# Turning the gathered slot rows by permuting loads and 32-by-32 block transposes in a fused attention and mixture-of-experts layer

## The chip, the core and the metric

The kernel runs on one core of a Trainium2 chip. Its metric is device time in microseconds, the median of several executions: 1471.43 us before the change, from three runs (1471.36 to 1472.84).

The core has five engines with queues of their own: TensorE (matrix products, from SBUF into PSUM), VectorE, ScalarE, GpSimd and SyncE, which here only issues transfers. They wait for each other through semaphores alone, and all of these waits are written out by hand.

## The reference

```python
x = layernorm(x + attention(x))          # 4 sequences x 512 tokens x 512 channels, 16 heads of 128
x_flat = x.reshape(2048, 512)
router_logits = x_flat @ w_router        # 8 experts
top_vals, top_idx = top_k(router_logits, 2)
probs = softmax(top_vals)
w_tok = zeros(2048, 8).at[rows, top_idx].add(probs)
h = square(relu(einsum("nc,ecd->ned", x_flat, w_fc)))     # every expert 512 x 512
y = einsum("ned,edc->nec", h, w_proj)
x = layernorm(x + einsum("nec,ne->nc", y, w_tok))
```

Attention has RMS norms on queries and keys, an ALiBi bias and a causal mask, a softmax, an RMS norm of the result and an output projection. The change touches only the experts' part. The inputs are fp32.

## The kernel before

**Attention** takes the first 965 us or so. After it comes **routing** in steps of 128 tokens (`token_steps`, 16 of them): project, add the residual, normalize, turn the tokens, route, rank within the expert. Each token's row is sent by GpSimd's indirect transfers (`dispatch`, line 952) to two slots of `slots_x` in HBM, and its two gate weights to `slots_g`.

**Slots.** A slot tile is 128 rows of 512 channels, all of one expert. Each expert has a region of tiles. 39 slot tiles are worked through (`SLOT_TILES`), expert by expert in "turns". The first turn belongs to the head expert, which is chosen after eight token tiles; its first two tiles (`HEAD`) are worked through while the last tokens are still being routed.

Precision: products are fp32r, with every fp32 operand split into a high part (ScalarE rounds it) and a low part (VectorE or GpSimd subtracts), and three products for each pair of blocks. So the product of a slot tile with a 512x512 matrix is 12 products of 128x128 by 128x512 (`times`, line 1641).

One slot step `k` has this order on the engines (`slot_step` in each of the functions `slots_*`):

- TensorE: turn the hidden rows of `k` (four identity products), the up product of tile `k+1`, turn the slot rows of tile `k+2` (`turn_x`, line 1635: four identity products into `turn_ps`), the down product of `k`.
- ScalarE: round the turned hidden rows of `k` (L1463), rectify the up product of `k+1` into `relu` (L1459), round the turned slot rows of `k+2` (`round_x`, L1454), scale the down product of `k` by the gates (L1469).
- VectorE: low part of the hidden rows of `k` (L1525), square of `k+1` (L1521, from `relu` and `relu` in SBUF), low part of the slot rows of `k+2` (`split_x`, L1516, from PSUM and `xt_hi`).
- SyncE: when the rows of `k+2` are turned, load the slot rows of `k+4` (`load_rows`, L1322, one transfer of 256 KB); then, when the output of `k` is ready, store it to `slots_y` (L1360) and load gates (L1325). The slot rows `xs` have two buffers.
- GpSimd: for each expert from the second on, load the raw weights (L1377) and the weights again as the later high part (L1383), 2 MB each, wait for both, and compute the low part in eight operations (L1392). A raw buffer holds one expert. After the last expert it gathers from `slots_y` into `x1` with indirect, adding transfers (L1422): 16 token tiles for the slot that comes first, then 16 for the second, each second pair of gathers after the output rows that it needs are stored (`rows_stored`, line 1414).

**The seam** between head and loop: VectorE computes tables of where each tile lies and which expert owns it (`slot_tables`), then `gates`, `row_shifts` (12 chained small operations, lines 1532 to 1548), `split_x(0, 3)`, `row_places` (lines 1554 to 1570), `square(0, 3)` and `split_x(1, 4)`. GpSimd begins to split the second expert's weights when `row_places` has ended (`slots_known`). SyncE loads tiles 2 and 3 when the tables are known and all dispatches have landed.

In the profile a tile's name is that of the first tensor at its place: `y_raw` holds `xs`, the hidden rows and the outputs; `turn_ps` holds the turned slot rows and the up products; `yt_hi` and `yt_lo` hold the high and low parts of slot and hidden rows; `x_nat` is `relu`.

## Time and profile before

| | |
|---|---|
| median of three runs | 1471.43 us (1471.36 to 1472.84) |
| span of the profiled execution | 1469.0 us (no time of its own is given beside it) |
| TensorE busy | 1428.9 us (97%), 7998 products |
| VectorE busy | 771.4 us (53%) |
| ScalarE busy | 727.3 us (50%) |
| GpSimd busy | 415.4 us (28%) |
| mean granted TensorE clock | 0.995 of full speed |
| slot row loads | 39 of 256 KB |
| transfers, share of 16 DMA engines | 31.2% hardware queue (SyncE), 12.0% software queue (GpSimd) |

The span runs from the first to the last instruction. The shares are means over stages with quite different limits: the DMA engines, for example, are 96% busy from 1386 to 1452 us and at 0.34 in the first 1030 us.

### The profile page before, as it was taken

What the parts mean: (1) busy time and instruction counts of PE and PEld (TensorE: products, weight loads), DVE (VectorE), ACT (ScalarE), POOL (GpSimd) and SP (SyncE); (2) the same over time, 40 slices, a digit from 0 to 9 for tenths busy, and PEclk for the clock granted to TensorE, in tenths of its full rate; (3) what the DMA queues carried; (4) which work ended last, traced back from release to release, by engine and by line L of the source; (5) the groups of instructions that cost most, each with busy time, mean ns of one, the idle gap of its engine ahead of it and who ended that gap; (6) DMA issues with size and microseconds to landing.
All of it is one profiled execution on the core that took longest, in us unless ns stands there. A gap on an engine that the chain in (4) does not pass through costs nothing. (4 is left out here: it accounts for less than half of the span.)

```text
span 1469.0 us, 26596 instructions
## 1 busy us (share of the span) xinstructions
PE 1428.9 (97%) x7998; PEld 1209.6 (82%) x7999; DVE 771.4 (53%) x1813; ACT 727.3 (50%) x1633; POOL 415.4 (28%) x410
## 2 busy tenths in 40 slices
PE   8999999999999999999999999989999989999994
PEld 6888888888888888888888888878888867888883
DVE  6555655655555655555555565545555563333334
ACT  5665655655656565556565565622222223333334
POOL 1212121212112212122121121103333445345575
PEclk9999999999999999999999999999999999999997
DMA  5243323232323333233323235433348446665699
GB/s 176 77 129 93 107 93 127 86 114 85 115 93 107 111 111 100 100 98 102 108 93 128 93 107 179 144 123 125 136 121 224 123 172 215 253 247 200 211 199 235
DMA packets 86547, 200.45 MB, mean 136 GB/s; under 512 B 15856, under 2 KB 16496, under 8 KB 83184
## 3 DMA queue, kind: packets, MB, share of 16 engines
q1 hardware_dynamic: 75728, 149.66, 31.2%
q0 software_dynamic: 10784, 50.36, 12.0%
q8 instruction: 18, 0.29, 0.1%
q14 instruction: 17, 0.14, 0.0%
HBM read 160.05 MB, written 92.62 MB: 172 GB/s over the span
## 5 line engine op out<-in xcount | busy, mean ns | idle before, releaser
L378 POOL TENSOR_TENSOR small<-small,half 128x4 f32<-128x4 f32 x193 | 194.9, 1010 | 768.8 <-DVE small L408 768.8
L511 DVE CUSTOM_DVE_ANT_0 logit<-score_ps,bias 128x128 f32<-128x128 f32 (+3 forms) x256 | 124.8, 487 | 157.0 <-PE score_ps L650 117.6
L312 ACT ACTIVATE prob<-logit,small 128x128 f32<-128x128 f32 (+3 forms) x256 | 144.2, 563 | 120.5 <-DVE small L511 116.8
L663 PEld LDWEIGHTS y_ps<-vs,prob_t 128*128 128x128 f32 x1280 | 175.0, 191 | 20.4 <-issue 3.7
L663 PE MATMUL y_ps<-vs,prob_t 128*128 (+1 forms) x1280 | 184.7, 275 | 0.3 <-DVE x_now L412 0.3
L319 ACT ACTIVATE prob_t<-prob_ps 128x128 f32<-128x128 f32 (+3 forms) x256 | 111.6, 436 | 54.4 <-PE prob_ps L656 53.4
L894 ACT ACTIVATE yt_hi<-turn_ps,subln 128x512 fp32r<-128x512 f32 x60 | 41.0, 688 | 154.1 <-PE turn_ps L1188 150.2
L656 PE MATMUL prob_ps<-ident,prob 128*128 128x128 f32 x640 | 112.7, 274 | 3.2 <-ACT prob L312 3.0
L576 PE MATMUL v_ps<-w_hi,x_hi 128*128 (+1 forms) x256 | 106.8, 417 | 1.3 <-DVE w_lo L447 1.3
L576 PE MATMUL v_ps<-w_hi,x_lo 128*128 (+1 forms) x256 | 106.3, 415 | 0.0
L576 PE MATMUL k_ps<-w_hi,x_hi 128*128 (+1 forms) x256 | 103.2, 403 | 0.6 <-DVE w_lo L447 0.6
L576 PE MATMUL q_ps<-w_hi,x_hi 128*128 (+1 forms) x256 | 102.4, 400 | 0.7 <-DVE w_lo L447 0.7
L576 PE MATMUL v_ps<-w_lo,x_hi 128*128 (+1 forms) x256 | 102.6, 401 | 0.0
L576 PE MATMUL k_ps<-w_lo,x_hi 128*128 (+1 forms) x256 | 101.7, 397 | 0.0
L576 PE MATMUL k_ps<-w_hi,x_lo 128*128 (+1 forms) x256 | 101.5, 397 | 0.0
L576 PE MATMUL q_ps<-w_hi,x_lo 128*128 (+1 forms) x256 | 101.3, 396 | 0.0
L576 PE MATMUL q_ps<-w_lo,x_hi 128*128 (+1 forms) x256 | 101.1, 395 | 0.0
L1392 POOL TENSOR_TENSOR w_lo<-w_raw,w_hi 128x512 f32 (+1 forms) x56 | 75.1, 1377 | 82.9 <-DMA w_hi<-in_w_experts 79.2
L656 PEld LDWEIGHTS prob_ps<-ident,prob 128*128 128x128 f32 x640 | 79.7, 141 | 14.3 <-ACT prob L312 7.1
L989 DVE SCALAR_TENSOR_TENSOR yt_lo<-turn_ps,subln,yt_hi 128x512 fp32r<-128x512 f32 x60 | 44.7, 749 | 85.3 <-ACT yt_hi L894 83.7
L240 ACT ACTIVATE ksq<-k_ps 128x512 f32<-128x512 f32 x64 | 38.4, 599 | 97.2 <-PE k_ps L576 97.2
L412 DVE TENSOR_TENSOR x_now<-y_ps,small 128x512 f32<-128x512 f32 x65 | 45.0, 692 | 77.4 <-POOL small L378 77.4
(250 smaller groups left out, 3421.5 us busy)
## 6 DMA issues: line engine op xcount, KB each, us to landing
slots_x<-in_zeros SPq DMA_DIRECT2D x64, 512.0 KB, 5.2
y_scratch<-x_now SPq DMA_DIRECT2D x65, 256.0 KB, 2.9
x_raw<-in_x_t SPq DMA_DIRECT2D x64, 256.0 KB, 2.8
slots_y<-in_zeros SPq DMA_DIRECT2D x64, 256.0 KB, 5.1
y_raw<-y_scratch SPq DMA_DIRECT2D x14, 1024.0 KB
w_raw<-in_w_experts POOLq DMA_DIRECT2D x7, 2048.0 KB
w_hi<-in_w_experts POOLq DMA_DIRECT2D x7, 2048.0 KB
w_raw<-in_w_all SPq DMA_DIRECT2D x16, 768.0 KB, 6.5
```

The costliest lines, as they stand in the source:

```text
L240: nc.scalar.activation(out[:, :, 0:D], src[:, :].rearrange("p (h d) -> p h d", h=HG), ACT.Square, scale=float(D) ** -0.5).then_inc(done, 1)
L312: nc.scalar.activation(prob[:, 0:width], logit[:, 0:width], ACT.Exp, scale=-1.0, bias=least[:, h:h + 1], accum_out=row_sum[:, (i % 2) * HG ...
L319: nc.scalar.activation(prob_t[:, 0:width], prob_ps[:, 0:width], ACT.Copy)\
L378: nc.gpsimd.tensor_tensor(r, ms, half[:, :], ALU.pow).then_inc(ready, 1)
L412: nc.vector.tensor_tensor(heads(out), heads(src[:, :]), r.unsqueeze(2).to_broadcast([P, HG, D]), ALU.mult).then_inc(done, 1)
L511: nc.vector.tensor_tensor_reduce(out=logit[:, 0:width], in0=score_ps[:, 0:width], in1=bias[:, h, T - width:T], scale=1.0, scalar=3e38, op0 ...
L576: mm = nc.tensor.matmul(out[:, :], xs, ws, start=(s == 0), stop=(s == 3 * CT - 1))
L656: mm = nc.tensor.transpose(prob_ps[:, j * P:(j + 1) * P], prob[:, j * P:(j + 1) * P], ident[:, :])
L663: mm = nc.tensor.matmul(y_ps[:, h * D:(h + 1) * D], prob_t[:, j * P:(j + 1) * P], one(vs[:, bass.ds(now, 1), j, h * D:(h + 1) * D]), start ...
L894: nc.scalar.activation(yt_hi[:, g, :], turn_ps[g][:, :], ACT.Copy, scale=subln[:, 0:1])\
L989: nc.vector.scalar_tensor_tensor(yt_lo[:, g, :], turn_ps[g][:, :], subln[:, 0:1], yt_hi[:, g, :], ALU.mult, ALU.subtract).then_inc(yt_read ...
L1392: nc.gpsimd.tensor_tensor(lo, w_raw[:, s, :], hi, ALU.subtract).then_inc(we_split, 1)
```

## The change

The slot rows no longer go through TensorE. A tile's load becomes four transfers, one for each quarter `u` of the channels. The transfer `u` puts into partition `32u + j` the 128 channels of quarter `u` of the rows `j`, `32 + j`, `64 + j` and `96 + j`. VectorE then transposes 32-by-32 blocks within each group of 32 partitions (`nc.vector.transpose`), and writes the blocks in the order that makes columns of 128 consecutive tokens (`turned_columns`). Partition `32u + j'` of column block `h` now holds channel `128u + 32h + j'`, so the up weights are laid out in that order on the host. The turned rows lie in a new SBUF tile `xt` in place of two PSUM banks; `round_x` and `split_x` read it there.

The order changes at these places. TensorE's `turn_x` is dropped in the head (twice), at the seam (twice) and in each slot step. VectorE gets it in the head ahead of each `split_x`, at the seam ahead of `row_shifts` and of `row_places`, and in the slot step between `split_hid` and `square`. In the head ScalarE waits for `last_projected` before it rounds the slot rows, since their high part lies where the last projection still reads. SyncE's wait on `xs_turned` is now on VectorE's operation.

```diff
--- before.py
+++ after.py
@@ -18,6 +18,8 @@
 AX = mybir.AxisListType
 
 P = 128
+QB = 4
+QP = P // QB
 B, T, C = 4, 512, 512
 H, D = 16, 128
 EPS = 1e-5
@@ -62,6 +64,11 @@
 def expert_block(e):
 
     return (CT + FT) * ((e + 2) % 3)
+
+
+def turned_columns(ap):
+
+    return ap.rearrange("p (h a j) -> p a h j", h=HG, a=QB)
 
 
 def one(ap):
@@ -849,7 +856,7 @@
 
         y_tiles = y_scratch[1:1 + NHG * NT, :, :].rearrange("(g t) p c -> t p g c", g=NHG)
         x_tiles = x_d.rearrange("(t p) c -> t p c", p=P)
-        x_slots = slots_x.rearrange("(k p) c -> k p c", p=P)
+        x_slots = slots_x.rearrange("(k a j) (u c) -> k u j a c", a=QB, j=QP, u=QB)
         LAST = NHG - 1
 
         def tile_of(tiles, t):
@@ -1272,13 +1279,15 @@
         end_rstd = sb("rstd3", [P, NT])
         minus_mean = sb("minus_mean", [P, NT])
 
-        xt_ps, h_ps = turn_ps[0:2], turn_ps[2:4]
+        h_ps = turn_ps[2:4]
+        xt = sb("xt", [P, 2, C])
         ht_ps, ye_ps = [out_ps[0], x1_ps], [out_ps[1], router_ps]
 
         end_set_up = sem("e_set_up")
         table_done = sem("slot_step")
         slots_known = sem("slots_known")
         g_loaded = [sem(f"g_loaded{y}") for y in range(YB)]
+        last_projected = sem("last_projected")
         we_cast = sem("we_loaded")
         xs_loaded = [sem("xs_loaded0"), sem("xs_loaded1")]
         xs_turned, xt_rounded, xt_ready = sem("xs_turned"), sem("xt_rounded"), sem("xt_ready")
@@ -1319,7 +1328,10 @@
                                      min_val=0, max_val=SPARE_TILE)
 
             def load_rows(at, b):
-                sp.dma_start(xs[:, b, :], rows_of(x_slots[bass.ds(at, 1), :, :])).then_inc(xs_loaded[b], 16)
+                for u in range(QB):
+                    sp.dma_start(xs[u * QP:(u + 1) * QP, b, :].rearrange("p (a c) -> p a c", a=QB),
+                                 x_slots[bass.ds(at, 1), u, :, :, :].rearrange("o j a c -> (o j) a c"))\
+                        .then_inc(xs_loaded[b], 16)
 
             def load_gates(at, y):
                 sp.dma_start(gs[:, y:y + 1], rows_of(g_slots[bass.ds(at, 1), :, :])).then_inc(g_loaded[y], 16)
@@ -1451,7 +1463,7 @@
 
             def round_x(b, count):
                 act.wait_ge(xs_turned, count)
-                nc.scalar.activation(xt_hi[:, b, :], xt_ps[b][:, :], ACT.Copy).then_inc(xt_rounded, 1)
+                nc.scalar.activation(xt_hi[:, b, :], xt[:, b, :], ACT.Copy).then_inc(xt_rounded, 1)
 
             def rectify(b, k):
                 act.wait_ge(up_done, k + 1)
@@ -1469,8 +1481,10 @@
                 nc.scalar.activation(yo[:, y, :], ye_ps[b][:, :], ACT.Copy, scale=gs[:, y:y + 1]).then_inc(yo_ready, 1)
 
             second_weight(NT - 3, 1)
+            act.wait_ge(last_projected, 1)
             round_x(0, 1)
             keep_x1(NT - 2, 0)
+            act.wait_ge(last_projected, 2)
             round_x(1, 2)
             second_weight(NT - 2, 0)
             act.wait_ge(summed, NT - 1)
@@ -1513,8 +1527,14 @@
 
             def split_x(b, count):
                 dve.wait_ge(xt_rounded, count)
-                nc.vector.tensor_tensor(xt_lo[:, b, :], xt_ps[b][:, :], xt_hi[:, b, :], ALU.subtract)\
+                nc.vector.tensor_tensor(xt_lo[:, b, :], xt[:, b, :], xt_hi[:, b, :], ALU.subtract)\
                     .then_inc(xt_ready, 1)
+
+            def turn_x(b, loaded, split=None):
+                dve.wait_ge(xs_loaded[b], loaded)
+                if split is not None:
+                    dve.wait_ge(xt_ready, split)
+                nc.vector.transpose(turned_columns(xt[:, b, :]), xs[:, b, :]).then_inc(xs_turned, 1)
 
             def square(b, count):
                 dve.wait_ge(relu_done, count)
@@ -1573,7 +1593,9 @@
             place(NT - 3, 1, 16 * NT - 64)
             gates(NT - 3, 1)
             layernorm(NT - 2, 0, 16 * NT - 32)
+            turn_x(0, 16 * QB)
             split_x(0, 1)
+            turn_x(1, 16 * QB)
             split_x(1, 2)
             choose(NT - 2)
             add_residual(NT - 1, 1, 8 * NT)
@@ -1586,14 +1608,18 @@
             place(NT - 1, 1, 16 * NT - 32)
             slot_tables(lambda: square(1, 2), lambda: split_hid(1, 1))
             gates(NT - 1, 1)
+            turn_x(0, 32 * QB, 1)
             row_shifts()
             split_x(0, 3)
+            turn_x(1, 32 * QB, 2)
             row_places()
             square(0, 3)
             split_x(1, 4)
 
             def slot_step(k, b, h, y, q):
                 split_hid(b, k)
+                if more(k, 2):
+                    turn_x(b, h * (16 * QB) + 32 * QB, k + 1)
                 if more(k, 1):
                     square(1 - b, k + 2)
                 if more(k, 2):
@@ -1632,12 +1658,6 @@
             scale_mean(NT - 2, NT)
 
         def slots_tensor(pe, project, turn_x1, route, rank, keep_busy):
-            def turn_x(b, loaded):
-                pe.wait_ge(xs_loaded[b], loaded)
-                for c in range(CT):
-                    mm = nc.tensor.transpose(xt_ps[b][:, c * P:(c + 1) * P], xs[:, b, c * P:(c + 1) * P], ident[:, :])
-                mm.then_inc(xs_turned, 1)
-
             def times(out, b, hi, lo, first_block, first=0, last=3 * CT):
 
                 for s in range(first, last):
@@ -1668,12 +1688,10 @@
 
             last = (NT - 1) * NHG
             pe.wait_ge(yt_ready, last + 1)
-            project(1, 0)
-            turn_x(0, 16)
+            project(1, 0).then_inc(last_projected, 1)
             pe.wait_ge(yt_ready, last + 2)
-            project(1, 1)
+            project(1, 1).then_inc(last_projected, 1)
             turn_x1(NT - 2, 0)
-            turn_x(1, 16)
             pe.wait_ge(yt_ready, last + 3)
             project(1, 2)
             route(NT - 2)
@@ -1698,19 +1716,15 @@
             times(ye_ps[0], 0, ht_hi, ht_lo, expert_block(0) + CT, 9, 12).then_inc(down_done, 1)
             pe.wait_ge(run_ready, NT + 1)
             down(1, 0, 1)
-            turn_x(0, 32)
             pe.wait_ge(tables_known, 2)
             second = load_owner(HEAD)
             keep_busy(h_ps[1], 10)
             up(0, second, 3)
-            turn_x(1, 32)
 
             def slot_step(k, b, h, y, q):
                 turn_hid(b, k)
                 if more(k, 1):
                     up(1 - b, load_owner(k + 1), k + 2)
-                if more(k, 2):
-                    turn_x(b, h * 16 + 32)
                 down(b, load_owner(k), k)
 
             slot_steps(pe, slot_step, HEAD)
@@ -1803,7 +1817,8 @@
     w_all = np.concatenate([qkv.transpose(3, 1, 2, 0, 4).reshape(W_ROUNDS, P, 3 * GW),
                             proj[:3 * CT].reshape(CT, 3, P, C).transpose(0, 2, 1, 3).reshape(CT, P, 3 * C)])
 
-    experts = np.concatenate([np.asarray(inputs["L0_ffn_w_fc"]).reshape(E, CT, P, F),
+    up = np.asarray(inputs["L0_ffn_w_fc"]).reshape(E, QB, CT, QP, F).transpose(0, 2, 1, 3, 4).reshape(E, CT, P, F)
+    experts = np.concatenate([up,
                               np.asarray(inputs["L0_ffn_w_proj"]).reshape(E, FT, P, C)], axis=1)
     bases = np.arange(E) * REGION_TILES * P
     floors = bases[:, None] + np.concatenate([[-1], P * np.arange(1, NT)])[None, :]
```

## Rows read from the trace of the kernel before

**Rows 1.** Chain that ended last, 1180 to 1469: start us, us, what

```profile
1317.58 2.79 PE turn_ps L1647 x12
1320.81 2.79 PE out_ps L1647 x12
...
1427.76 2.97 DMA slots_y<-y_raw
```

**Rows 2.** Time line of GpSimd: start us, us, engine, line, operation

```profile
1209.84 10.88 POOL L1392 TENSOR_TENSOR w_lo<-w_raw,w_hi 128x512 fp32r<-128x512 f32 x8 [3.66 <-DVEq L1570]
...
1373.94 10.51 POOL L1392 TENSOR_TENSOR w_lo<-w_raw,w_hi 128x512 f32 x8 [13.51 <-DMA w_hi<-in_w_experts]
1386.64 1.68 POOL L1422 DMA_INDIRECT x<-slots_y,slot_y  x1 [2.19 <-issue]
...
1420.97 1.56 POOL L1422 DMA_INDIRECT x<-slots_y,slot_y  x1 [1.67 <-issue]
...
1427.07 1.54 POOL L1422 DMA_INDIRECT x<-slots_y,slot_y  x1 [2.68 <-issue]
...
1451.06 1.54 POOL L1422 DMA_INDIRECT x<-slots_y,slot_y  x1 [0.30 <-issue]
```

**Rows 3.** Time line of VectorE near the end

```profile
1453.79 0.16 DVE L1615 SCALAR_TENSOR_TENSOR minus_mean<-mean_var,rstd 128x4 f32<-128x4 f32 x1 [1.07 <-POOL rstd L1428]
```

**Rows 4.** Time line of VectorE at 1179

```profile
1178.86 0.55 DVE L1009 TENSOR_SCALAR x_now<-res,mean_var,rstd 128x512 f32<-128x512 f32 x1
```

**Rows 5.** Three lines of code: count, ns min/median/max, first and last start

```profile
L1521 DVE TENSOR_TENSOR y_raw<-x_nat x39: 691/693/1684, 1191.9 to 1443.8; 128x512 f32<-128x512 f32 x39
L1516 DVE TENSOR_TENSOR yt_lo<-turn_ps,yt_hi x39: 676/682/692, 1179.3 to 1437.9; 128x512 fp32r<-128x512 f32 x39
L1392 POOL TENSOR_TENSOR w_lo<-w_raw,w_hi x56: 1259/1292/1753, 1209.8 to 1383.2; 128x512 f32 x40, 128x512 fp32r<-128x512 f32 x16
```

**Rows 6.** Time line of SyncE's queue, loads of slot rows

```profile
1163.96 0.91 SPq L1322 DMA_DIRECT2D y_raw<-slots_x  x2
...
1202.90 1.44 SPq L1322 DMA_DIRECT2D y_raw<-slots_x  x2
```

**Rows 7.** Time lines of TensorE, then VectorE, at the seam

```profile
1205.58 0.66 PE L1638 MATMUL turn_ps<-ident,y_raw 128*128 128x128 f32 x4 [0.68 <-DMA y_raw<-slots_x]
...
1207.97 0.49 PE L1647 MATMUL turn_ps<-w_hi,yt_hi 128*128 x1 [0.23 <-issue]
...
1202.95 0.39 DVE L1532 TENSOR_TENSOR beyond<-slot,bases 128x224 f32<-128x224 f32 x1
...
1205.81 0.25 DVE L1548 SCALAR_TENSOR_TENSOR place_y<-slot,first_ahead,shift 128x32 f32<-128x32 f32 x1
...
1207.58 0.17 DVE L1554 TENSOR_TENSOR slot_y<-place_y 128x16 uint32<-128x16 f32 x1
...
1209.19 0.51 DVE L1568 TENSOR_SCALAR due<-due_f,end_tile 128x16 int32<-128x16 f32 x2
```

**Rows 8.** Time line of one slot step, 1245 to 1250

```profile
1245.86 0.60 PE L1662 MATMUL x_ps<-ident,y_raw 128*128 128x128 f32 x4
...
1246.64 0.59 ACT L1463 ACTIVATE yt_hi<-x_ps 128x512 fp32r<-128x512 f32 x1
...
1247.27 0.69 DVE L1525 TENSOR_TENSOR yt_lo<-x_ps,yt_hi 128x512 fp32r<-128x512 f32 x1 [1.95 <-ACT yt_hi L1463]
...
1249.92 0.69 DVE L1521 TENSOR_TENSOR y_raw<-x_nat 128x512 f32<-128x512 f32 x1 [1.96 <-ACT x_nat L1459]
```

**Rows 9.** DMA queues, 1252:1262 then 1397:1425: packets, MB, share of 16 engines

```profile
q0 software_dynamic: 246, 3.77, 89.6%
q1 hardware_dynamic: 217, 0.41, 11.6%
...
q0 software_dynamic: 1856, 3.38, 74.2%
q1 hardware_dynamic: 1998, 2.35, 26.6%
```

## The prediction

> **What bounds the kernel now.** I read the busy table first: TensorE works 97% of the span at full clock, so the first question is what sets its order. The chain of waits shows it in the slot loop: blocks of 12 products of 2.79 us that start 3.23 us apart [rows 1]. The 0.44 us between them are the four identity products of a turn, one for the hidden rows and one for the slot rows, in alternation. A slot step is therefore 2 x 3.23 = 6.46 us. But the chain leaves TensorE at the end: it goes over a store of slot rows (2.97 us) into GpSimd's gathers. So TensorE's order decides up to about 1427 us and GpSimd's after it, and I read GpSimd's time line next [rows 2]. It begins its first weight split at 1209.84, its seventh at 1373.94 (27.35 us per expert), and its first gather at 1386.64. Those starts follow loads and splits, never TensorE. GpSimd then has some slack: 18 gathers at 1.845 us each take 33.2 us, and the 19th starts at 1427.07, 40.4 us after the first. GpSimd can thus come 7.2 us later before the end moves. Past 1427 it issues without a gap to 1451.06, and VectorE's last statistics had to wait 1.07 us for GpSimd's power behind those gathers [rows 2, 3].
>
> **Filled tiles.** The reference's routing of these inputs gives the experts 5, 4, 5, 4, 4, 5, 5 and 4 tiles, 36 of 39. The head is the third expert, so turns begin at tiles 0, 5, 9, 14, 18, 22, 27 and 32. Tile 33 releases the gather at 1427.07; the last three tiles hold nothing.
>
> **What is removed.** 39 turns of four identity products leave TensorE. Two of them lie before the seam, 2 x 0.44 = 0.9 us, and all that follows the last projection comes 0.9 us earlier. 35 lie in the loop: if TensorE stayed the bound, 35 x 0.44 = 15.4 us.
>
> **What a turn costs on VectorE.** No transpose of VectorE is in the trace. The nearest operations on 128x512 fp32 are 0.55 us (a scale from SBUF to SBUF) and, as the long end, 1.68 us (the slowest squaring) [rows 4, 5]. I take 0.69, an unhindered pass, and keep both ends.
>
> ScalarE's two new waits, on the last projection of the first two head groups, cost nothing: TensorE was past both when it turned these rows, and the rounding came after.
>
> **The seam.** The load of tile 2 is issued at 1202.90, held by the last dispatch, and lands at 1205.58, 2.68 us later [rows 6, 7]. It will be issued at 1202.0. Now it is four transfers, and issues stand about 0.57 us apart (two in 0.91 us, the second lasting 0.34): the fourth leaves at 1203.7 and lands at 1206.4. VectorE has the new turn ahead of row_shifts, and there it waits for the load. The 12 chained small operations of row_shifts (1202.95 to 1206.06), which lay beside the load, come behind it: turn to 1207.1, row_shifts 3.1 us to 1210.2, split to 1210.9, first product at 1211.1. Before, that product stood at 1207.97, so TensorE is 3.1 us late. The second turn is put ahead of row_places (1207.58 to 1209.70, 2.1 us): 1210.9 + 0.7 + 2.1 = 1213.7, and GpSimd, which waits for slots_known, starts splitting at 1213.85 in place of 1209.84. That is 4.0 us on GpSimd's whole chain [rows 2, 7]. TensorE has part of its delay back since the third tile's turn is gone too: I put up(5) at 1229.3 (before 1226.8).
>
> **The loop.** The new step is 0.44 + 2.79 + 2.79 = 6.02 us. On the path from one hidden turn to the up products two halves on, the times behind the end of the hidden turn (1246.46) are: its rounding and split done at +1.5, the new turn at +2.2, the rectified rows at +3.4 (+3.6 with waits), square, split_x [rows 8]. Alone these end at +5.0 of 6.02: hidden. Beside GpSimd's splits they don't. The squaring reads two SBUF tiles and took up to 1.68 us; the splits that read PSUM never exceeded 0.69 [rows 5]. split_x now reads xt and xt_hi, both in SBUF, so it joins the squaring. The squaring starts within a GpSimd operation of 1.29 us and waits half of one; split_x right behind it meets the next one: 3.6 + 1.3 + 1.9 = +6.8 to +7.0. That is 0.9 us late per step, in the 1.8 steps of each split, 7 x 1.8 x 0.9 = 11 us. Of 28 x 0.44 = 12.3 us almost nothing is left, and up(32) is at 1229.3 + 27 x 6.02 + 11 = 1402.8, before 1401.6.
>
> GpSimd pays too. Eight operations at the least 1.259 are 10.07 us; the first split took 10.88 with two squarings within it, so 0.4 us for each [rows 2, 5]. 12.6 more such meetings add 5.4 us. A lower bound is nothing, the upper 0.69 for each.
> By the Trainium skill ("SBUF — State Buffer", section "SBUF: two separate sides") the pair of ports is held for a whole instruction and the loser fully blocks; by that each meeting would cost GpSimd 0.69 us and the sum 8.7 instead of 5.4. The squaring's stretched times agree with a lock, the 0.4 us does not bear out the full length.
>
> **The transfers.** A slot tile was 128 packets of 2 KB; now it is 512 of 512 B. While weights load, both queues are served by packet, not by byte: in 10 us 246 packets of 16 KB on GpSimd's queue and 217 of SyncE's [rows 9]. In the gather stretch too: 1856 beside 1998 in 28 us with the engines full. SyncE's queue has 1998/28 x 6.46 = 461 packets per step; the change adds 384 and 48 completions: 893, at 71 per us 12.5 us, twice a step. In the loop the 16 us between two weight loads clear the backlog, and a load made during one lands when the weights do, within the two steps that it has. For the weights themselves: SyncE's 217 packets took 11.6% of the engines in those 10 us, 0.085 us each; a quarter of the bytes each would free up to 0.9 us per load, twice as many packets' time would add 1.2. I take 0.15 less, 1 us in six loads. SyncE's three more issues per step (3 x 0.57 us) fall where it waits for the output rows, over 3 us a step, and hold nothing.
> The Trainium skill ("DMA: Bandwidth & Descriptors", section "Specifications") gives 512 B as the least transfer at line rate. By it the smaller pieces cost nothing in the stretches where engines are free, and it says nothing of two queues that take turns; by it alone the sum would be that of the first rival below.
>
> **The end, summed.** GpSimd's first gather comes 4.0 + 5.4 - 1.0 = 8.4 us later, at 1395.0. Up(32) at 1402.8 puts the turns of tiles 32, 33, 34 and 35 at 1398.2, 1404.2, 1410.2 and 1416.2, and each releases the load of the tile two on. Tile 34's (issued 1398.2) takes 576/71 = 8.1 us and the landing's 2, so 1408.5: in time. Tile 35's queues behind 288 packets of stores and gates (4.1 us) and takes 8.1 more, so 1421 where 1417.6 would still be hidden (the turn may come 1.4 us late before the squaring wants VectorE). Tile 36's ends with the first list's traffic, at 1432.5. The store of tile 33 (issued 1424.7) stands behind tiles 36 and 37 in the same queue and lands at 1434.5. Gather 19 therefore starts at 1435.5 against 1427.07: +8.4, and the 13 behind it, the statistics and the normalization follow as before. Slots end on VectorE at 1454 (before 1447.8), +6, covered. The profiled span goes from 1469.0 to 1477.4. The profiled execution has no time of its own beside its span; the median run is 2.4 above that span, and the same 2.4 gives 1479.8. I say 1479.
>
> **Rivals.**
> 1. The queue does not starve (four pieces of one row count as one packet, or gathers leave room). Then 8.4 - 7.2 = 1.2 us later: 1472.6. For it: TensorE never waited in that stretch so far. Against: the packet counts are equal in two stretches of very different sizes.
> 2. Faster: split_x does not meet GpSimd (it falls between its operations), or weights come sooner since small packets take less of each turn. GpSimd is then 4.0 late or less, below the 7.2 of slack, and TensorE leads: 2.5 late at up(5), less 12.3, so tile 33 comes 9.8 earlier and the gathers 7.2 - 4.0 = 3.2 earlier: 1468.2. It decides wherever GpSimd's delay stays under 7.2 us.
> 3. All 37 x 0.44 = 16.3 us: 1455. Only if the seam hides too and GpSimd's chain shortens by 9 us or more, for which no row speaks.
> 4. Late loads in the weight stretches as well: a load that is issued as the weights start has 576 packets at 22 per us and comes with the end of the weights, 2 us late, six times: 12 us on top, 1491.
>
> **How the numbers follow.** Forecast 0.45 (its own range 1475 to 1487), rival 1 0.22, rival 2 0.15, rival 3 0.05, rival 4 0.13. What this kernel's measurement can tell from no change is about 0.2%, 2.9 us. Faster by more: rival 3, most of rival 2 and an edge of rival 1, 0.19. Within: most of rival 1, 0.20. Slower: 0.61. The range leaves out rival 3, the far end of rival 2 and the far end of rival 4: 1466 to 1492.
>
> **What would show it.** Right: the first product of tile 2 near 1211, GpSimd's first split near 1213.9; that split at 11.3 us or more; split_x with a maximum near 1.9 us; the turn at 0.7; first gather near 1395; in the gathers GpSimd waiting on a store of slot rows, and VectorE's turn waiting on loads. Wrong: a first gather before 1391, loop blocks at 3.0 us apart throughout, or no wait for slot rows after 1400.

## The result and the profile after

The changed kernel takes 1477.78 us (median of 6 runs, 1476.52 to 1484.32); the kernel before took 1471.74 beside it (1468.96 to 1473.17). The ratio is 1.0052 (95% interval 1.0038 to 1.0066): slower by 0.5%, and 1479 was forecast. The profiled execution took 1481.32 us for a span of 1479.7, so it lies 3.5 above its median. That matters below: its routing ran 1.6 to 1.8 us later than in the trace of before, ahead of anything that changed at the seam (the first load of `x_nat` in routing is at 967.95 against 966.35, the last at 1164.09 against 1162.26).

The page of the changed kernel: the span, busy times, the granted clock in 40 slices, and the chain that ended last by engine.

```profile
span 1479.7 us, 26713 instructions
...
PE 1420.5 (96%) x7842; PEld 1198.3 (81%) x7843; DVE 807.5 (55%) x1852; ACT 728.5 (49%) x1633; POOL 419.5 (28%) x410
...
PEclk9999999999999999999999999999999989999997
```

156 identity products are gone, yet TensorE is only 8.4 us less busy. The new `8` in the clock row is the slice of the seam.

The three lines of code beside [rows 5] (count, ns min/median/max), of the changed kernel:

```profile
L1537 DVE STREAM_TRANSPOSE xt<-y_raw x39: 695/702/714, 1181.2 to 1445.7; 128x512 f32<-128x512 f32 x39
L1530 DVE TENSOR_TENSOR yt_lo<-xt,yt_hi x39: 677/684/1777, 1182.6 to 1448.4; 128x512 fp32r<-128x512 f32 x39
L1404 POOL TENSOR_TENSOR w_lo<-w_raw,w_hi x56: 1253/1293/1782, 1218.3 to 1397.7; 128x512 f32 x40, 128x512 fp32r<-128x512 f32 x16
```

The turn costs 0.70 us, and the split of the slot rows, never over 0.69 before, now reaches 1.78.

GpSimd's time line, beside [rows 2]: start, us, then in brackets the idle time before and what ended it.

```profile
1218.33 10.79 POOL L1404 TENSOR_TENSOR w_lo<-w_raw,w_hi 128x512 fp32r<-128x512 f32 x8 [11.27 <-DVEq L1590]
...
1388.05 10.94 POOL L1404 TENSOR_TENSOR w_lo<-w_raw,w_hi 128x512 f32 x8 [13.16 <-DMA w_hi<-in_w_experts]
1401.17 1.68 POOL L1434 DMA_INDIRECT x<-slots_y,slot_y  x1 [2.19 <-issue]
...
1414.09 1.53 POOL L1434 DMA_INDIRECT x<-slots_y,slot_y  x1 [2.03 <-issue]
...
1438.05 1.54 POOL L1434 DMA_INDIRECT x<-slots_y,slot_y  x1 [0.86 <-issue]
...
1462.03 1.54 POOL L1434 DMA_INDIRECT x<-slots_y,slot_y  x1 [0.30 <-issue]
```

The first split is 8.5 us later than before, the first gather 14.5, the nineteenth and the last 11.0. The pause of 2.03 us ahead of the seventh gather fits a wait for TensorE's rows, though the view names no releaser: it starts 5.6 us behind the issue of a store (1408.47), as the nineteenth does (1432.45).

**The seam.** SyncE's issues of tiles 2 and 3, then VectorE's time line beside [rows 7]:

```profile
1204.11 4.90 SPq L1332 DMA_DIRECT2D y_raw<-slots_x  x8
```

```profile
1211.15 0.71 DVE L1537 STREAM_TRANSPOSE xt<-y_raw 128x512 f32<-128x512 f32 x1 [7.07 <-DMA y_raw<-slots_x]
1211.78 0.35 DVE L1552 TENSOR_TENSOR beyond<-slot,bases 128x224 f32<-128x224 f32 x1
...
1214.59 0.25 DVE L1568 SCALAR_TENSOR_TENSOR place_y<-slot,first_ahead,shift 128x32 f32<-128x32 f32 x1
1214.88 0.69 DVE L1530 TENSOR_TENSOR yt_lo<-xt,yt_hi 128x512 fp32r<-128x512 f32 x1
1215.48 0.70 DVE L1537 STREAM_TRANSPOSE xt<-y_raw 128x512 f32<-128x512 f32 x1
1217.68 0.51 DVE L1588 TENSOR_SCALAR due<-due_f,end_tile 128x16 int32<-128x16 f32 x2
```

VectorE stands idle for 7.07 us ahead of the turn, and both `row_shifts` and `row_places`, for which GpSimd waits, stand behind it.

Five stretches of the changed kernel: us, busy time (instructions) of TensorE, its weight load, VectorE, ScalarE and GpSimd, then the granted clock, the DMA share and GB/s.

```profile
1205.00:1210.00 5.00, 2.03 (x14) 1.56 (x13) 0.00 (x0) 0.00 (x0) 1.76 (x2) 1.00 0.27 60
1210.00:1215.00 5.00, 0.00 (x0) 0.00 (x0) 3.44 (x14) 1.21 (x2) 0.00 (x0) 0.50 0.24 49
1215.00:1220.00 5.00, 4.11 (x10) 3.25 (x11) 2.94 (x12) 0.00 (x0) 1.67 (x2) 0.50 0.34 106
1220.00:1225.00 5.00, 1.99 (x9) 1.24 (x8) 3.40 (x4) 1.71 (x3) 5.00 (x4) 0.84 0.33 104
1225.00:1230.00 5.00, 5.00 (x13) 3.89 (x13) 0.51 (x1) 0.00 (x0) 4.12 (x4) 0.50 0.20 52
```

TensorE ran ten filler products and then nothing for some 9 us. Its granted clock fell from 1.00 to 0.50, that is from 2.4 to 1.2 GHz. It fell twice: within 1220 to 1225 (0.84 in the mean) it was back at 1.00, from the last products of the first dozen on, and dropped again at about 1223.7, after TensorE had waited from 1220.9 with only four identity products in between. At 1225 to 1230 the engine needed 5 us for 13 products. The kernel before has 1.00 in all of 1205 to 1225.

**The chain of waits** of the changed kernel, beside [rows 1]:

```profile
1206.04 5.08 DMA y_raw<-slots_x
1211.15 0.71 DVE xt L1537
...
1215.89 5.06 PE turn_ps L1667 x12
...
1222.61 1.69 DVE yt_lo L1530
...
1224.60 5.48 PE turn_ps L1667 x12
...
1263.44 12.67 DMA y_raw<-slots_x
...
1322.42 10.23 DMA y_raw<-slots_x
...
1347.92 11.99 DMA y_raw<-slots_x
...
1393.56 1.78 DVE yt_lo L1530
...
1426.06 2.79 PE turn_ps L1667 x12
1428.85 2.80 PE router_ps L1667 x12
1431.65 0.44 PE out_first L1682 x4
...
1450.68 3.84 DMA slots_y<-y_raw
```

Where nothing hinders it, the loop runs as forecast: 0.44 + 2.79 + 2.80 = 6.03 us a step, on to 1450 at least. But three loads of 10 to 13 us and stretched splits lie on the chain. The waits of 1215 to 1460 sum them up (us in total, times, longest):

```profile
POOL w_lo L1404 <- DMA w_hi<-in_w_experts: 82.3, 6, 14.9
...
PE turn_ps L1667 <- DVE yt_lo L1530: 18.2, 11, 8.9
...
DVE xt L1537 <- DMA y_raw<-slots_x: 6.7, 4, 3.3
```

DMA queues of the changed kernel in a stretch of weight loads (1262 to 1272) and in one of gathers (1403 to 1431), beside [rows 9]:

```profile
q0 software_dynamic: 234, 3.57, 95.9%
q1 hardware_dynamic: 188, 0.02, 2.2%
...
q0 software_dynamic: 1872, 3.42, 73.9%
q1 hardware_dynamic: 3827, 2.40, 29.8%
```

**One clock for all kernels.** The runs differ ahead of the seam by up to 7 us, so I compare profiled executions from the issue of tile 2's load on. All times are in us behind it; "out k" is the time at which ScalarE begins to scale the output rows of tile k, "loop" is out 33 minus out 2 (31 steps, 186.9 at 6.03), and the gathers count from GpSimd's first.

| kernel | first up product | out 2 | loop | out 33 | first split | eight operations x7 | gather 1 | gather 19 | end of span |
|---|---|---|---|---|---|---|---|---|---|
| before | 5.1 | 17.3 | 200.3 | 217.6 | 6.9 | 75.1 | 183.7 | 224.2 | 266.1 |
| after | 11.8 | 29.1 | 198.5 | 227.6 | 14.2 | 78.6 | 197.1 | 233.9 | 275.6 |
| e1_seam | 9.7 | 24.6 | 203.5 | 228.1 | 5.1 | 78.7 | 195.6 | 234.7 | 276.6 |
| e2_psum | 11.7 | 26.8 | 193.8 | 220.7 | 14.1 | 75.8 | 193.6 | 228.8 | 271.8 |
| e3_one_load | 7.5 | 23.6 | 197.1 | 220.6 | 9.9 | 79.6 | 193.7 | 229.4 | 272.0 |
| e4_seam_psum | 9.5 | 24.0 | 198.1 | 222.2 | 5.2 | 74.5 | 189.9 | 228.7 | 271.8 |
| b1_four_loads | 9.4 | 22.8 | 207.0 | 229.9 | 11.2 | 76.3 | 195.0 | 235.4 | 277.3 |
| b2_split_sbuf | 5.0 | 19.8 | 208.6 | 228.4 | 6.9 | 78.6 | 193.5 | 234.3 | 276.6 |
| e5_busy | 11.5 | 27.6 | 198.1 | 225.7 | 13.9 | 78.6 | 195.2 | 232.6 | 275.2 |
| e6_four_buffers | 11.1 | 27.5 | 188.7 | 216.2 | 13.5 | 75.2 | 194.0 | 228.6 | 271.2 |
| e8_psum_one | 7.6 | 23.9 | 187.7 | 211.6 | 10.0 | 74.9 | 187.6 | 223.0 | 264.8 |
| e9_gates_late | 8.5 | 33.5 | 205.3 | 238.8 | 14.0 | 76.7 | 206.6 | 245.7 | 288.4 |
| b3_places | 6.5 | 18.6 | 201.1 | 219.7 | 5.5 | 75.1 | 184.5 | 225.4 | 267.0 |
| e7_all | 8.2 | 21.4 | 190.2 | 211.6 | 5.4 | 74.9 | 183.3 | 218.1 | 260.0 |

Each row is one execution. Before and after end 9.5 us apart on this clock; the difference of their medians, with the 0.9 us by which the issue should come earlier, is 6.9. Over all rows the median less the end of the span lies between 1202.2 and 1205.9, so a difference of 1 to 2 us between two rows is not resolved.

**Two chains meet at gather 19.** One is TensorE's, through the store of tile 33, and it leads where gather 19 comes 5.5 to 6.7 us behind out 33: in before, after, e1, e4, b1, b2 and b3. The other is GpSimd's, from gather 1, and it leads in e2, e3, e6 and e8: there the nineteenth is 34.6 to 35.7 us behind the first, and 8 to 12 us behind out 33. In e5 and e7 the two all but meet: gather 19 is 6.9 and 6.5 us behind out 33. In the changed kernel GpSimd alone would put gather 19 near 197.1 + 35 = 232, and TensorE puts it at 233.9. So both chains are late, TensorE's by 9.8 us and GpSimd's by about 8: mending TensorE's alone can bring back some 2 us (the pause ahead of gather 7 is 1.7 above the usual 0.30), mending GpSimd's alone nothing. That governs how each experiment reads.

### The profile page after: what moved, and what is told of

Read it like the earlier page. It is cut to its first block and busy times, and to the rows that moved or that the text cites. A ratio compares the mean times of both kernels' runs of the same rounds, so it can differ in the third digit from the quotient of the medians.

```text
span 1479.7 us, 26713 instructions
## 1 busy us (share of the span) xinstructions
PE 1420.5 (96%) x7842; PEld 1198.3 (81%) x7843; DVE 807.5 (55%) x1852; ACT 728.5 (49%) x1633; POOL 419.5 (28%) x410
## 5 line engine op out<-in xcount | busy, mean ns | idle before, releaser
L1404 POOL TENSOR_TENSOR w_lo<-w_raw,w_hi 128x512 f32 (+1 forms) x56 | 78.6, 1437 | 93.5 <-DMA w_hi<-in_w_experts 82.3
```

Source lines behind the costliest of these rows:

```text
L1404: nc.gpsimd.tensor_tensor(lo, w_raw[:, s, :], hi, ALU.subtract).then_inc(we_split, 1)
```

## The experiments

The theory I started from: the change loses at four places, at the seam through VectorE's order and the four pieces, in the loop through `split_x` beside GpSimd, and through loads that come late while weights load. The rivals give the loop's loss to one of the last two alone, or the seam's to TensorE's clock.

**e1_seam**, the new turns behind both table steps:

```diff
-            turn_x(0, 32 * QB, 1)
             row_shifts()
+            row_places()
+            turn_x(0, 32 * QB, 1)
             split_x(0, 3)
             turn_x(1, 32 * QB, 2)
-            row_places()
```

> The changed kernel with row_shifts and row_places ahead of the first turn at the seam, so that they lie beside the load of tile 2 instead of behind it. GpSimd's first split should start at about 1209.5 in the time line of the changed kernel in place of 1218.3, TensorE's first product of tile 2 at 1213.3 in place of 1215.9. Theory (GpSimd's chain and TensorE's chain meet at the store of tile 33, both nearly binding): only TensorE's 2.6 us come back, 1475 us. Rival (GpSimd's chain alone sets the end): about 8 us come back, 1470 us.

1482.17 us, ratio 1.0063 (1.0038 to 1.0087) to before: nothing gained. Yet GpSimd began 9.1 us earlier (first split at 5.1 for 14.2) and out 2 was 4.5 earlier. GpSimd's time line in e1 shows why that did not pay:

```profile
1402.60 2.19 POOL L1434 DMA_INDIRECT x<-slots_y,slot_y  x1 [8.99 <-DMA slots_y<-y_raw]
```

GpSimd was early and waited 8.99 us for the store of tile 27: TensorE's chain bound alone, and its loop was 5 us longer (203.5). That the splits and weight loads now met other steps would explain it, but was not tried by itself. It shows again in e2 and e4 (193.8 and 198.1), but hardly with four buffers for slot rows (e6 188.7, e7 190.2), and VectorE waited longer for loads in the loop (10.8 us in e1 for 6.7 in the changed kernel), which speaks for the late loads. So the seam order costs both chains, 9.1 us at GpSimd's first split and 2.1 at TensorE's first product, and mending it alone gains nothing, since the loop takes it back.

**e2_psum**, the turned rows in PSUM again, as four edits of one kind (dots stand for code left out, here and below):

```diff
-        h_ps = turn_ps[2:4]
-        xt = sb("xt", [P, 2, C])
+        xt_ps, h_ps = turn_ps[0:2], turn_ps[2:4]
...
-                nc.scalar.activation(xt_hi[:, b, :], xt[:, b, :], ACT.Copy).then_inc(xt_rounded, 1)
+                nc.scalar.activation(xt_hi[:, b, :], xt_ps[b][:, :], ACT.Copy).then_inc(xt_rounded, 1)
...
-                nc.vector.tensor_tensor(xt_lo[:, b, :], xt[:, b, :], xt_hi[:, b, :], ALU.subtract)\
+                nc.vector.tensor_tensor(xt_lo[:, b, :], xt_ps[b][:, :], xt_hi[:, b, :], ALU.subtract)\
...
-                nc.vector.transpose(turned_columns(xt[:, b, :]), xs[:, b, :]).then_inc(xs_turned, 1)
+                nc.vector.transpose(turned_columns(xt_ps[b][:, :]), xs[:, b, :]).then_inc(xs_turned, 1)
```

> The changed kernel with VectorE's transposes writing into the two PSUM banks that held the turned rows before, so that split_x has one SBUF source again. Theory (split_x fights with GpSimd's splits): split_x never over 0.70 us, TensorE's 18.2 us of waits for it mostly gone, GpSimd's eight operations back to 10.5 to 10.9 us per expert, 3.5 us in all; with GpSimd nearly binding 3 to 4 us come back, 1474 us. Rival (the meeting costs nothing on the path): 1478 us. Second rival: the transposes into PSUM are themselves slower than 0.70 us.

1475.00 us, ratio 1.0028 (1.0014 to 1.0042). The two lines of code in e2:

```profile
L1536 DVE STREAM_TRANSPOSE turn_ps<-y_raw x39: 716/718/728, 1176.9 to 1434.8; 128x512 f32<-128x512 f32 x39
L1529 DVE TENSOR_TENSOR yt_lo<-turn_ps,yt_hi x39: 675/684/692, 1178.4 to 1437.5; 128x512 fp32r<-128x512 f32 x39
```

The turn costs 0.02 us more and the split never stretches. The loop falls by 4.7 us (193.8), GpSimd's operations by 2.8 (78.6 to 75.8). VectorE's wait for loads rose from 6.7 to 10.3 us over the same stretch: by that, a part of the late loads had been hidden behind the stretched splits.

**e3_one_load**, the slot rows in one transfer of 256 KB (rows in plain order, so the turned rows are not those of the reference; the waits are a quarter as high):

```diff
-                for u in range(QB):
-                    sp.dma_start(xs[u * QP:(u + 1) * QP, b, :].rearrange("p (a c) -> p a c", a=QB),
-                                 x_slots[bass.ds(at, 1), u, :, :, :].rearrange("o j a c -> (o j) a c"))\
-                        .then_inc(xs_loaded[b], 16)
+                sp.dma_start(xs[:, b, :], rows_of(x_slots[bass.ds(at, 1), :, :])).then_inc(xs_loaded[b], 16)
```

> The changed kernel with one transfer of whole 2 KB rows per tile, without the permutation of quarters, which is left out. Theory (pieces of 512 B cost at the seam and in the weight stretches): VectorE's first turn near 1207 in place of 1211.2, no wait of VectorE for slot rows in the loop in place of 13.8 us in five waits; both chains 4 us earlier at the seam and GpSimd's waits for weights back from 82.3 to about 79 us: 1471 us. Rival (the pieces are harmless): 1478 us.

1474.98 us, 1.0035 (1.0019 to 1.0051). The seam gives back 4.3 us at the first product and as much at the first split. The loop alone shortens by 1.4 (197.1), with `split_x` still in SBUF. Late loads did not vanish with the pieces, as had been expected: VectorE still waits 4.2 us for slot rows in the loop, in three waits, for 6.7 in four.

**e4_seam_psum**, the edits of e1 and e2 together.

> The seam order of the first run and the PSUM target of the second together. Theory of two chains: GpSimd is 12 us earlier than in the changed kernel, TensorE 2.6 from the seam and up to 10 from split_x, less what late loads keep: 6 to 9 us come back, 1470 us, which is the time before the change or slightly less. Rival (gains of the two do not add, since late loads hold TensorE): 1474 us.

1474.20 us, 1.0010 (0.9991 to 1.0029). First split at 5.2, `split_x` clean, loop 198.1, and gather 19 6.5 us behind out 33: TensorE's chain binds, held by the seam's load and the late loads.

**b1_four_loads**, the kernel before with the four-piece load alone (the view `x_slots` as in the changed kernel and waits four times as high, not shown; the rows so loaded are not in the order that its turns assume):

```diff
-                sp.dma_start(xs[:, b, :], rows_of(x_slots[bass.ds(at, 1), :, :])).then_inc(xs_loaded[b], 16)
+                for u in range(4):
+                    sp.dma_start(xs[u * 32:(u + 1) * 32, b, :].rearrange("p (a c) -> p a c", a=4),
+                                 x_slots[bass.ds(at, 1), u, :, :, :].rearrange("o j a c -> (o j) a c"))\
+                        .then_inc(xs_loaded[b], 16)
```

> The kernel before with its loads of slot rows cut in the four pieces of the change, and nothing else; the rows are then turned as they lie, so the order of channels is left wrong. Theory (late pieces hold whoever turns): the load of tile 2 lands about 4 us later at the seam, TensorE waits for slot rows in the weight stretches, 1477 to 1480 us. Rival (pieces are harmless where TensorE's step is 6.46 us): 1471.7 us.

1482.05 us, 1.0081 (1.0052 to 1.0110). Out 2 is 5.5 later and the loop 6.7 longer. TensorE's waits in 1215 to 1460 of b1:

```profile
PEld turn_ps L1641 <- DMA y_raw<-slots_x: 5.0, 5, 1.3
...
PE turn_ps L1641 <- DMA y_raw<-slots_x: 2.8, 5, 0.9
```

Both lines tell of the same five waits, first on the weight load and then on the products, so they do not add; the trace of before has none of them in this stretch. TensorE's products stand idle for 2.8 us in them, and behind each the work restarts some 0.7 us slower (0.66 us for four identity products in place of 0.44, a gap of 0.25, 3.04 for 2.79 in the dozen): together about the 6.7 us. Late loads cost the loop by themselves.

**b2_split_sbuf**, the kernel before with `split_x` reading an SBUF tile (the low part is then that of other data):

```diff
-                nc.vector.tensor_tensor(xt_lo[:, b, :], xt_ps[b][:, :], xt_hi[:, b, :], ALU.subtract)\
+                nc.vector.tensor_tensor(xt_lo[:, b, :], x_nat[:, 1, :], xt_hi[:, b, :], ALU.subtract)\
```

> The kernel before, in which the low part of the slot rows is computed from another SBUF tile of the same size in place of PSUM (its values are left wrong). Only the second SBUF source is added. Theory (two SBUF sources meet GpSimd's splits): that subtraction up to 1.8 us long, GpSimd's splits 3.5 us longer in all, which its 7.2 us of slack cover, TensorE up to 0.5 us late in some 12 steps: 1474 to 1477 us. Rival (no cost on the path): 1471.7 us.

1481.37 us, 1.0064 (1.0043 to 1.0085). The split of b2, and what TensorE waited for it from 1215 to 1460:

```profile
L1516 DVE TENSOR_TENSOR yt_lo<-x_nat,yt_hi x39: 678/687/1782, 1179.2 to 1449.0; 128x512 fp32r<-128x512 f32 x39
```

```profile
PE turn_ps L1647 <- DVE yt_lo L1516: 6.5, 11, 1.3
```

The loop is 8.3 us longer and GpSimd's operations 3.5. One changed operand does that. b1 and b2 keep the identity products, so they show the two costs without the gain: 10.2 and 9.6 us between medians, where the whole change costs 6.0.

**e5_busy**, 75 filler products for 10 ahead of tile 2's up product, against the clock:

```diff
-            keep_busy(h_ps[1], 10)
+            keep_busy(h_ps[1], 75)
```

> The changed kernel with 75 in place of 10 idle-filling identity products between the last product of the head and the first of tile 2. Theory (TensorE's clock fell to half since it stood idle for 9 us at the seam, and the products of tiles 2 and 3 took 5.1 and 5.5 us per dozen in place of 3.1): the granted clock stays at full, the first two dozens take 3.1 us each, 4 to 5 us come back: 1473 us. Rival (the lost time lies in the waits alone): 1478 us.

1478.77 us, 1.0048 (1.0033 to 1.0064), as the changed kernel. The chain of e5 at the seam:

```profile
1216.51 3.07 PE turn_ps L1667 x12
...
1224.00 5.48 PE turn_ps L1667 x12
```

The first dozen has its 3.07 us back, but the clock fell in the 4.4 us between the two, in which TensorE ran only four identity products, and the second took 5.48 as before. Out 2 came 1.5 earlier.

**e6_four_buffers**, e2 with four buffers for slot rows, each load issued two tiles sooner (the second pair of buffers, their semaphores and the loads of tiles 4 and 5 at the seam are not shown):

```diff
-                if more(k, 4):
+                if more(k, 6):
                     sp.wait_ge(xs_turned, k + 3)
                     sp.nop(nofuse=True)
-                    load_rows(at, b)
+                    load_rows(tile_at(k + 6), (y + 2) % YB)
```

> The kernel with the PSUM target, and four buffers for slot rows in place of two, so that a load starts four tiles ahead of its turn instead of two. Theory (loads that are late in the weight stretches hold TensorE, but with the PSUM target GpSimd's chain already sets the end): VectorE's waits for slot rows in the loop gone, the loop from the store of tile 2 to that of tile 33 from 193.7 to about 187.5 us, and the time hardly lower than that kernel's 1475.0 us: 1473 to 1475. Rival (TensorE's chain still sets the end): 1469 us.

1473.69 us, 1.0015 (1.0001 to 1.0028). The loop is 188.7, 1.8 above its floor of 186.9, and out 33 is before that of the kernel before. Gather 19 is 34.6 behind gather 1: GpSimd's chain binds, since the seam still starts it 6.6 late. e6 is e1's mirror.

**e8_psum_one**, e2 and e3 together.

> The PSUM target with one transfer of whole rows per tile (the permutation of quarters is left out). Theory (of the loop's lost 12 us about half is split_x against GpSimd and half the pieces): from the store of tile 2 to that of tile 33 187 to 189 us, against 198.4 in the changed kernel, 193.7 with the PSUM target alone and 197.0 with one transfer alone; the end is set by GpSimd, 1471 to 1474 us. Rival (the two costs hide behind one another): the loop stays near 193 us.

1468.74 us, 0.9988 (0.9974 to 1.0002). The loop is 187.7. With after, e2 and e3 this makes the square: 198.5 with both losses, 193.8 without the split's, 197.1 without the pieces', 187.7 without either. Taking the split out of SBUF brings 4.7 or 9.4, taking the pieces out 1.4 or 6.1, the smaller number while the other loss is there. Each is one profiled execution, so the 1.4 by itself is within what two rows can differ by; the 4.7, 6.1 and 9.4 are not.

**e9_gates_late**, GpSimd's last scatter of gate weights moved behind the seam:

```diff
-            send_gates(NT - 1, 1)
             pool.wait_ge(slots_known, 2)
+            send_gates(NT - 1, 1)
```

> The changed kernel with GpSimd's last scatter of gate weights put behind the end of row_places, so that it no longer runs while the pieces of tile 2 are in flight. Theory (the pieces land 7.0 us after the first is issued, since the scatter's 4-byte packets hold the engines for about 3 us): the first turn of VectorE at the seam 3 us earlier, 4 us after the first piece is issued, and TensorE's first product of tile 2 8.8 us after it in place of 11.8. Rival (four issues and the strided pieces take 7 us by themselves): no change in these two. GpSimd's first split comes 2.5 us later than it would otherwise in either case.

One execution, 1490.31 us (before 1470.56): the late gates hold the scaling of tile 2 (out 2 at 33.5), so its total says nothing. What it was built for is VectorE's turn at the seam, with the load issued at 1200.35:

```profile
1204.14 0.71 DVE L1537 STREAM_TRANSPOSE xt<-y_raw 128x512 f32<-128x512 f32 x1 [3.80 <-DMA y_raw<-slots_x]
```

The turn starts 3.8 us behind the first issue, where it was 7.0, and the first product 8.5, where it was 11.8. So 3.2 of the seam's 4.4 us of later landing are not the pieces as such, but pieces in flight while GpSimd's scatter of 4-byte elements runs.

**e7_all**: e1, e2 and e6 together, with 45 filler products.

> PSUM target, seam order with row_shifts and row_places ahead, four buffers, and 45 idle-filling products at the seam: every cost that was found is taken off, except the four pieces and their late landing at the seam. Theory: GpSimd's first gather comes as early, counted from the load of tile 2, as in the kernel before (184 us), TensorE's store of tile 33 5 to 8 us earlier, and the gathers run without a wait: 3 to 5 us below the time before, 1467 to 1469 us. Rival (the late pieces and GpSimd's chain eat it all): 1472 us.

1465.89 us, 0.9957 (0.9942 to 0.9972), faster than both kernels. GpSimd's time line in e7:

```profile
1206.16 10.35 POOL L1408 TENSOR_TENSOR w_lo<-w_raw,w_hi 128x512 fp32r<-128x512 f32 x8 [2.18 <-DVEq L1594]
...
1384.12 1.68 POOL L1438 DMA_INDIRECT x<-slots_y,slot_y  x1 [2.19 <-issue]
...
1443.14 1.54 POOL L1438 DMA_INDIRECT x<-slots_y,slot_y  x1 [0.30 <-issue]
```

**b3_places**, the kernel before with `row_places` ahead of `split_x`, as a control for e7:

```diff
             row_shifts()
-            split_x(0, 3)
             row_places()
+            split_x(0, 3)
```

> The kernel before, with row_places moved ahead of the first split_x at the seam, as in the best kernel so far; TensorE still turns the slot rows. GpSimd starts its splits up to 0.9 us earlier, the low part of tile 2 comes up to 2 us later. Theory (before the change TensorE's chain, over the store of tile 33, sets the end, so that an earlier GpSimd is worth nothing): the time stays or rises by up to 2 us, 1471 to 1474 us, and the gain of the best kernel is due to the removed identity products. Rival (the best kernel's gain is the seam order, and would be had without the change): 1466 to 1468 us.

1472.34 us, 1.0010 (0.9999 to 1.0022). The seam order by itself gives the old kernel nothing. More fillers and four buffers were not tried in the old kernel; its trace has a clock of 1.00 at the seam and no wait for slot rows from 1215 on, so nothing there speaks for a gain from them. With that left open, e7's 0.43% is what the removed identity products give once their side effects are covered: out 2 is 4.1 us later than before, the loop 10.1 shorter, and out 33 and gather 19 thus 6 us earlier.

## Why the prediction came right, step by step

1479 forecast, 1477.8 measured, inside the range and on the forecast side. It came right by luck: two errors of 8.3 and 7.4 us cancelled, one term that was mis-sized and one whose mechanism did not occur. On the clock of the table, from the issue of tile 2's load to gather 19 (the forecast puts that issue at 1202.0):

| term | forecast | measured |
|---|---|---|
| TensorE late at the seam | +3.4 | +11.7 |
| 31 steps of the loop | -1.3 | -1.8 |
| loads starved in the gather stretch | +2.2 | 0 |
| store of tile 33 to gather 19 (5.8 before) | +5.0 | -0.2 |
| gather 19 | +9.3 | +9.8 |

The forecast's column: up(5) at 1229.3 for 1226.8 and the issue 0.9 earlier; 11 less 28 x 0.44 = 12.3; the store of tile 33 at 1424.7 for 1421.3, so 4.3 on this clock, of which the first two terms are 2.1; its gather at 1435.5, 10.8 behind the store. (The trace of before has up(5) at 1227.1 and not at 1226.8, and from there to up(32) are 27 steps and not 28; the two slips cancel.) Measured, the store is issued at 1432.45 and the gather 5.6 behind it. The 8.3 us that the seam cost beyond its price stand against 7.4 of starvation that did not come.

**The seam was mis-sized**, 3.4 for 11.7. The order of the wait was right: turn, `row_shifts`, split, product. What was off: the pieces land at 7.0 us, not 4.4. Issues stand 0.62 us apart for the 0.57 taken; the rest, 2.6 us in all, goes with the scatter of gate weights (e9), which I had not looked for, although it is issued 0.9 us behind the load in the trace of before too (1203.81). The forecast priced everything at full clock, and the clock halved, twice: two dozens at 5.06 and 5.48 us, 4.4 us above those that follow at 3.06. e5's fillers had back 2.0 of the 4.4. And the squaring and `split_x` of the third and fourth tile stood beside GpSimd's first split (1.69 us on the chain for 0.69), where I had priced the loop's contention but not the seam's. The three are 2.6 + 4.4 + 1.0 = 8.0 of the 8.3 us. GpSimd's start was off for the first of these reasons: +7.3 for +4.9 on this clock (4.0 and the 0.9).

**GpSimd's chain.** Its operations grew by 3.5 us, for 5.4 forecast (12.6 meetings at 0.4 us are 5.0, so 0.4 of this is a slip in the sum). b2, where one operand alone was moved into SBUF, gives the same 3.5, so the price is that of `split_x` meeting GpSimd; e2, without it, is at 75.8 again. The meetings cost VectorE far more: single splits went from 0.69 us to 1.78, and all 39 together from 26.6 us to 37.3 (39.8 in b2). The Trainium skill ("SBUF — State Buffer", section "SBUF: two separate sides") has the later one blocked for the whole instruction of the other; by that and the forecast's 12.6 meetings GpSimd would have lost up to 8.7 us, an estimate. The trace agrees that the two hold each other up, and the 3.5 us (0.28 a meeting) say that VectorE was mostly the one that waited. The slack of 7.2 us was too large as well: it took 18 gathers at 33.2 us, and where GpSimd leads they take 34.6 to 35.7. The saving of 1 us on weight loads was wrong in sign: the waits for weights went from 79.2 to 82.3 us. It is not the pieces: they are 82.3 in e3 without them and 77.5 in b1 with them. The cause stays open.

**The loop was right in size, and its cause only half.** I gave the whole 11 us to `split_x` beside GpSimd and held late loads in the weight stretches for a rival (12 us on top, 0.13). Both mechanisms act, and they hide behind one another: a step that waits for its load has its split late anyway. e2, e3 and e8 show 10.8 us for both together, 4.7 and 1.4 for each alone. Three of six weight stretches put a load on the chain. So rival 4 was real and not additive.

**The starvation after 1400 did not come**, and it was the term with the most arithmetic behind it. I had read equal packet counts in [rows 9] as a rule of service. It held again with 16 KB packets (234 beside 188; 161 packets of that stretch are under 512 B, too small for slot rows, so the tile's pieces stood behind them, and 998 packets passed in the 2 us from 1274 on, when the weights were in). It failed in the gathers: 3827 packets of SyncE's queue passed beside 1872, at the same megabytes as before (2.40 and 2.35). TensorE kept its 6.03 us step there. That the counts had once been alike at 1856 and 1998 would then be a coincidence of demand: the queue had asked for no more. What makes the two stretches differ was not tried.

**Rivals.** 1 (no starvation, 1472.6) had its mechanism right and fell to the seam. 2 (GpSimd within its slack, TensorE leads, 1468.2): TensorE did lead in the end, but because it was late. 3 (all 16.3 us) is out of reach: e7 kept 6, with the seam still 4.1 late and both chains meeting at gather 19. In medians e7 kept 5.0 us. Of the signs named ahead, `split_x` at 1.78, the turn at 0.70 and the waits for loads came; the first product (1215.9 for 1211), the first split (1218.3 for 1213.9; 10.8 long for 11.3) and the first gather (1401.2 for 1395) were later than named, and no load was late in the gather stretch. The last was one of the signs that I had named for being wrong: the time came right although its mechanism, in this part, did not.

## What to carry to other kernels

When work moves off the bounding engine, list each chain that meets the end with its own lateness: here two were late by 8 and 10 us, so e2 and e3, the best single repairs, brought back 3 of the 6 us, and only the repairs together beat the kernel before. A packet count that is equal once in a trace is a share only if the queue was asking for more; check that before it is made a rule. And where a change opens idle stretches of TensorE like the two here, of 9 and 4 us, price the work behind them at half clock too.

## What was not expected of the hardware

- A block transpose of 128x512 fp32 on VectorE with permuted blocks takes 0.70 us from SBUF to SBUF and 0.72 into PSUM, and was not slowed beside GpSimd (maximum 0.714).
- TensorE's granted clock went from 1.00 to 0.50 over an idle stretch of 9 us, was back at 1.00 for 1221 to 1223, and fell again over some 4 us with only four identity products in them (in e5 this second fall came alike); 12 products of 128x128 by 128x512 behind such a stretch then took 5.1 to 5.5 us for 3.06.
- A subtraction of VectorE on 128x512 with both sources in SBUF lost 10.7 us over 39 (13.2 in b2) to GpSimd's splits, which themselves lost 3.5 over 56; with one source in PSUM (e2) they stood at 26.7 us for 26.6 before, and at 75.8 for 75.1.
- Four loads of 64 KB in pieces of 512 B landed 7.0 us behind the first issue beside a scatter of 4-byte elements and 3.8 without it (e9, one execution); one load of 256 KB took 2.7 (before, e3).
- Of two queues, SyncE's passed 188 packets beside 234 of GpSimd's with 16 KB each (10 us), but 3827 beside 1872 with 2 KB each (28 us).
